# Transposing the probabilities of four heads in three chunks, the shared head put together by the transfer queue

## The reference

```
# layer 0
q, k, v = x @ Wq.T + bq, y @ Wk.T + bk, y @ Wv.T + bv
x1 = softmax(where(mask == 0, -1e9, q @ k.T)) @ v + x
# layer 1, 16 heads of 32
Q, K, V = x1 @ Wq.T + bq, ctx @ Wk.T + bk, ctx @ Wv.T + bv
attn = softmax(Q_h @ K_h.T / sqrt(32))          # for each head, 77 keys
out = LayerNorm(concat_h(attn @ V_h) @ Wo.T + bo + x1) * gamma + beta
```

## Time and profile before

| | us |
|---|---|
| median of 3 runs | 410.09 |
| lowest, highest of them | 408.79, 412.2 |
| the profiled execution, its own time | 408.65 |
| span of the profile | 406.8 |

### The profile page before, as it was taken

The page is one execution under the profiler, slowest core; times in us unless marked ns, Lnnn a source line. Parts: engine busy times, 40 slices in busy tenths (PEclk is TensorE's granted clock), DMA queues, the critical chain, the costliest instruction groups (busy, mean ns, idle before and its releaser), DMA issues.

```text
span 406.8 us, 12216 instructions
## 1 busy us (share of the span) xinstructions
PE 390.2 (96%) x4984; PEld 298.0 (73%) x4984; DVE 292.8 (72%) x711; ACT 260.7 (64%) x780; POOL 221.4 (54%) x244
## 2 busy tenths in 40 slices
PE   8999998899999999999999999999999999999894
PEld 8869856577777877777777777677777777777663
DVE  0456477548867898678967986778867986657787
ACT  2333678765678674867578567857588558766820
POOL 0420377225547755776567754765478654763541
PEclk9999999999999999999999999999999999999998
DMA  8885003400032301421041303240042200251022
GB/s 301 305 312 210 12 3 118 136 3 3 2 129 86 131 2 28 171 95 56 2 162 54 131 2 122 93 131 2 3 161 97 88 2 16 81 174 61 2 105 103
DMA packets 17302, 37.56 MB, mean 92 GB/s; under 512 B 1808, under 2 KB 3344, under 8 KB 16223
## 3 DMA queue, kind: packets, MB, share of 16 engines
q1 hardware_dynamic: 16815, 36.24, 26.0%
q10 hardware_dynamic: 432, 0.54, 0.4%
HBM read 26.49 MB, written 8.39 MB: 86 GB/s over the span
## 4 chain that ended last, share of the span: by engine, by line
PE 83%; ACT 11%; DVE 2%; DMA 2%; issue 1%; SPq 0%; DVEq 0%
PE ps_q L958 22%; PE ps_out L1023 20%; PE ps_t L983 14%; PE ps_s L972 7%; PE ps_pv L998 6%; PE ps_out L918 5%; ACT prob L503 3%; ACT pt L512 3%; ACT y L524 2%; PE ps_s L884 2%; PE ps_s L1041 2%; ACT q L467 1%; PE ps_s L897 1%; DMA raw<-in_w0k 1%; PE ps_t L1086 1%
## 5 line engine op out<-in xcount | busy, mean ns | idle before, releaser
L360 POOL TENSOR_TENSOR prob<-prob,rc 128x308 f32<-128x308 f32 x128 | 91.2, 719 | 126.0 <-DVE rc L712 125.8
L503 ACT ACTIVATE prob<-ps_s,mx 128x77 f32<-128x77 f32 x512 | 121.9, 324 | 1.8 <-DVE mx L703 1.8
L512 ACT ACTIVATE pt<-ps_t 77x512 f32<-77x512 f32 x128 | 76.2, 595 | 61.4 <-PE ps_t L983 60.9
L710 DVE TENSOR_REDUCE sm<-prob 128x4 f32<-128x308 f32 x128 | 59.5, 465 | 37.0 <-ACT prob L503 36.8
L983 PE MATMUL ps_t<-ident,prob 128*77 128x128 f32 x512 | 79.2, 277 | 3.1 <-ACT pt L512 3.1
L983 PEld LDWEIGHTS ps_t<-ident,prob 128*77 128x77 f32 x512 | 61.6, 147 | 21.5 <-issue 7.6
L703 DVE TENSOR_REDUCE mx<-ps_s 128x4 f32<-128x308 f32 x128 | 53.9, 469 | 23.1 <-PE ps_s L972 23.1
L335 POOL TENSOR_TENSOR x_l<-x_raw,x_h 128x512 fp32r<-128x512 f32 x32 | 44.6, 1398 | 21.9 <-ACT x_h L449 11.7
L958 PE MATMUL ps_q<-x_h,wq_h 128*128 128x512 f32 x128 | 53.2, 415 | 0.0
L958 PE MATMUL ps_q<-x_h,wq_l 128*128 128x512 f32 x128 | 53.0, 414 | 0.0
L972 PEld LDWEIGHTS ps_s<-k1T,q 32*64 32x64 f32 x2048 | 25.8, 130 | 27.8 <-issue 15.0
(11 more groups left out here) (130 smaller groups left out, 605.4 us busy)
## 6 DMA issues: line engine op xcount, KB each, us to landing
x_raw<-in_xT SPq DMA_DIRECT2D x8, 1024.0 KB, 7.4
y<-in_x SPq DMA_DIRECT2D x28, 256.0 KB, 2.7
out<-y SPq DMA_DIRECT2D x28, 256.0 KB, 2.0
mask_sb<-in_mask SPq DMA_DIRECT2D x8, 154.0 KB, 7.3
raw<-in_w0q SPq DMA_DIRECT2D x4, 256.0 KB, 5.9
raw<-in_w0v SPq DMA_DIRECT2D x1, 1024.0 KB, 10.1
raw<-in_w1q SPq DMA_DIRECT2D x1, 1024.0 KB, 12.7
raw<-in_w1k SPq DMA_DIRECT2D x1, 1024.0 KB, 5.0
```

Source lines behind the costliest of these rows:

```text
L360: nc.gpsimd.tensor_tensor(ap, ap, wide(rc[:, k % 2, h], KEYS), ALU.mult).then_inc(prob_done, 1)
L503: e = nc.scalar.activation(prob[:, k % 2, h, t], ps_s[:, h, t * KEYS:(t + 1) * KEYS], ACT.Exp, bias=mx[:, k % 2, h, t:t + 1])
L512: nc.scalar.activation(pt[:, h], ps_t[0:KEYS, :], ACT.Copy).then_inc(pt_ready, 1)
L710: nc.vector.reduce_sum(sm[:, k % 2, h], prob[:, k % 2, h], AX_X).then_inc(sum_done, 1)
```

## The change

The probabilities of a unit are laid out tile, head, key, so that the 4 x 77 = 308 columns of a tile lie side by side. For units 0 to 30 they are transposed as three chunks of 128, 103 and 77 columns (`CHUNK`) and not as four heads of 77. Chunk 0 holds head 0 and the first 51 keys of head 1; chunk 1 holds the other 26 keys of head 1 and then head 2; chunk 2 is head 3. Chunk c waits for POOL's scaling of head c + 1. ACT copies three chunks and not four heads.

Head 1 lies in two chunks. Two transfers on SP's queue (`gather`) bring its parts together in a new tile `pt_1`: 51 partitions from chunk 0, 26 from chunk 1. `context` waits for both (`pt_moved`). Head 2 starts 26 partitions down in chunk 1; its values are put 26 rows down in a new tile `v1_2` with zeros above, so that its matmul contracts 103 rows. `v1_2` is zeroed by POOL and filled by two transfers at the start, for which PE waits in step 1 (`v1_moved`). SP's program becomes a step for each unit too, with the same transfers as before at other places. The last unit keeps four groups of 77 columns, and copies head 1 straight to `pt_1`.

```diff
+SPLIT = P - KEYS
+CHUNKS = 3
+CHUNK = ((0, P), (P, 3 * KEYS), (3 * KEYS, GCOLS))
+SHIFT = 2 * KEYS - P
+SHIFTED = SHIFT + KEYS
...
-        pt = sb("pt", [KEYS, KC, BLOCK])
-        prob = sb("prob", [P, 2, GROUP_HEADS, TILES, KEYS])
+        pt = sb("pt", [P, CHUNKS, BLOCK])
+        pt_1 = sb("pt_1", [KEYS, BLOCK])
+        prob = sb("prob", [P, 2, TILES, GROUP_HEADS, KEYS])
...
+            sp.wait_ge(v1_ready, BATCH)
+            by_heads = v1[:].rearrange("p b (g h d) -> p b g h d", h=GROUP_HEADS, d=HEAD_DIM)
+            for v in range(BATCH):
+                sp.dma_start(v1_2[SHIFT:SHIFTED, v], by_heads[:, v, :, 2]).then_inc(v1_moved, 16)
+
+            def gather(i, k, c):
+                if not unit_exists(i, k) or k == UNITS - 1:
+                    return
+                wait(sp, pt_ready, chunks(i, k, c) + 1)
+                if c == 0:
+                    sp.dma_start(pt_1[0:SPLIT], pt[KEYS:P, 0]).then_inc(pt_moved, 16)
+                else:
+                    sp.dma_start(pt_1[SPLIT:KEYS], pt[0:SHIFT, 1]).then_inc(pt_moved, 16)
+
+            def step(i, k):
+                g, b = k % CH, k // CH
+                gather(i, k - 1, 0)
+                if g == 3:
+                    stack_probs(i, b + 1)
+                gather(i, k - 1, 1)
+                if k == 1:
+                    stack_weights(u_a, u_b, slice(1, 2), u_stacked[1], u_ready, 2)
...
+                    for t in range(TILES):
+                        load_rows(i, 0, t)
+                if g == 3:
+                    next_inputs(i, b + 1)
+                    store(i, b - 1, 0)
...
+                if g == 0:
+                    store(i, b - 2, 1)
+                if g == 1:
+                    store(i, b - 2, 2)
+                    store(i, b - 2, 3)
+                if b > 1 and k < UNITS:
+                    if g < 2:
+                        load_rows(i, b - 1, g)
+                    if g == 2:
+                        load_rows(i, b - 1, 2)
+                        load_rows(i, b - 1, 3)
...
-            def transposes(i, k, h):
+            def transposes(i, k, c):
...
-                wait(pe, prob_done, heads(i, k, h) + 1)
-                wait(pe, pt_ready, heads(i, k, h))
+                wait(pe, prob_done, heads(i, k, c + 1) + 1)
+                wait(pe, pt_ready, chunks(i, k, c))
+                n = CHUNK[c][1] - CHUNK[c][0]
                 for t in range(TILES):
-                    mm = nc.tensor.transpose(ps_t[0:KEYS, t * P:(t + 1) * P], prob[:, k % 2, h, t], ident[:])
+                    cols_of = prob[:, k % 2, t].rearrange("p h k -> p (h k)")[:, CHUNK[c][0]:CHUNK[c][1]]
+                    mm = nc.tensor.transpose(ps_t[0:n, t * P:(t + 1) * P], cols_of, ident[:])
                 mm.then_inc(t_done, 1)
...
+                if k < UNITS - 1:
+                    wait(pe, pt_ready, chunks(i, k, CHUNKS))
+                    wait(pe, pt_moved, 32 * (units(i, k) + 1))
+                    pairs = ((values(0), pt[0:KEYS, 0]), (values(1), pt_1[:]),
+                             (v1_2[:, b % 2, g], pt[0:SHIFTED, 1]), (values(3), pt[0:KEYS, 2]))
...
                 if type(i) is int and k == 1:
                     pe.wait_ge(v1_ready, BATCH)
+                    pe.wait_ge(v1_zero, 1)
+                    pe.wait_ge(v1_moved, 32)
                 transposes(i, k - 1, 0)
...
-                transposes(i, k - 1, 3)
```

More of the change, by code:

```diff
@@ L184, in units, with chunks @@
             return TURN * i + k
+        def chunks(i, k, c):
+            return CHUNKS * units(i, k) + c
         def heads(i, k, h):
@@ L265, in stored_rows, with store @@
                 return beta_done, TILES * b + t + 1
-            def store(i, b):
+            def store(i, b, t):
                 if not block_exists(i, b):
                     return
[L271 to L276, removed]
+                wait(sp, *stored_rows(b, t))
+                sp.dma_start(out[b % 2, i + b // 2, t], y[:, t, :]).then_inc(stored[t], 16)
             def move(to, frm, done):
@@ L302, in _ @@
             stack_weights(v0_a, v0_b, slice(0, BATCH), v0_stacked, v0_ready, BATCH)
[L304 to L315, removed]
+            sp.wait_ge(v1_ready, BATCH)
[18 more added lines that the diff above has]
+                    stack_weights(u_a, u_b, slice(1, 2), u_stacked[1], u_ready, 2)
+                    sp.wait_ge(mm_u, BATCH)
+                    sp.wait_ge(wq_ready, 2)
+                    sp.wait_ge(wq_l_ready, 2)
+                    for t in range(TILES):
[3 more added lines that the diff above has]
+                    store(i, b - 1, 0)
+                if g == 3 and b == LAST - 1:
                     sp.wait_ge(xl_ready, CH * BLOCKS)
@@ L319, in _ @@
                     sp.dma_start(last_y[:], last_x.rearrange("t p d -> p t d")).then_inc(ld_last, 16)
-                store(0, b - 2)
+                if g == 0:
[9 more added lines that the diff above has]
+                        load_rows(i, b - 1, 3)
+            for k in range(STEPS):
+                step(0, k)
             for t in range(TILES):
@@ L530, in step @@
                     round_ct(i, k - 2)
-                leave_pt(i, k - 1, 0)
+                transposed(i, k - 1, 0)
                 exps(i, k, 0)
@@ L534, in step @@
                     round_p0(i, b + 1)
-                leave_pt(i, k - 1, 1)
+                transposed(i, k - 1, 1)
                 exps(i, k, 1)
@@ L991, in context, with values @@
                 wait(pe, ctl_ready, units(i, k))
-                wait(pe, pt_ready, heads(i, k, GROUP_HEADS))
                 if g == 2 and block_exists(i, b + 1):
                     wait(pe, p0l_ready, blocks(i, b + 1) + 1)
-                for h in range(GROUP_HEADS):
-                    rows_of = slice(h * HEAD_DIM, (h + 1) * HEAD_DIM)
-                    own = slice(g * P + h * HEAD_DIM, g * P + (h + 1) * HEAD_DIM)
-                    mm = nc.tensor.matmul(ps_pv[rows_of, :], v1[:, b % 2, own], pt[:, h], start=True, stop=True)
+                def values(h):
+                    return v1[:, b % 2, g * P + h * HEAD_DIM:g * P + (h + 1) * HEAD_DIM]
+                if k < UNITS - 1:
[3 more added lines that the diff above has]
+                             (v1_2[:, b % 2, g], pt[0:SHIFTED, 1]), (values(3), pt[0:KEYS, 2]))
+                else:
+                    wait(pe, pt_ready, chunks(i, k, GROUP_HEADS))
+                    pairs = ((values(0), pt[0:KEYS, 0]), (values(1), pt_1[:]),
+                             (values(2), pt[0:KEYS, 1]), (values(3), pt[0:KEYS, 2]))
+                for h, (w, v) in enumerate(pairs):
+                    mm = nc.tensor.matmul(ps_pv[h * HEAD_DIM:(h + 1) * HEAD_DIM, :], w, v, start=True, stop=True)
                 mm.then_inc(pv_done, 1)
```

47 lines of the change are left out of this document (34 added, 13 removed).

## The result

| | before | after |
|---|---|---|
| median, us (20 runs each) | 410.4 | 408.26 |
| ratio of the runs, 95% interval | | 0.9908 (0.9881 to 0.9934) |
| profiled execution, own time | 408.65 | 406.01 |
| its span | 406.8 | 404.2 |
| mean granted clock | 0.996 | 0.984 |

The change gains 0.9%, 3.8 us by the ratio. The ratio leaves out runs that lie over 1.5% above the fastest of their kernel (two of 484 us before; after, six from 410.07 to 412.89 and one of 934.45), so it leans to the side of the change: the medians of all runs are only 2.1 us apart. I had forecast 401.2. The ranges of the runs overlap: the lowest after is 403.79.

The account below looks back on a forecast made before the run. PE, busy 96% of the span, was taken as the bound. The terms -12.0 + 2.0 + 1.3 + 0.6 = -8.1 took 408.65 to 400.5, 401.2 as a median; range 396.5 to 406.5.

Parts of the forecast that it names:

- What a group costs: Units 3 to 30: each dropped group of four transposes saves 0.43 us of PE, 28 x 0.43 = -12.0 us.
- What the wider chunks cost: Transposes of 128 and 103 columns: their longer weight loads fit the pace of 0.11 us, so 0.
- The wait for the moved rows in ordinary steps: Before the context: the 26 partitions land 2.0 to 3.5 us after issue, under the 4.04 of room; 0.
- the step I took for the tightest: Step 16, with g = 0: 4.47 us from ACT's second copy to the context, 4.04 without the fourth group.
- The start, unit 0: First transposes wait for two transfers of moved values, landing at 52.4: +2.0 us (1.3 to 2.8, up to 4).
- the rivals: Gate of the clock: falling to 1.2 GHz in unit 0's wait costs some 2 us more, 403.2; chance 0.2.
- Unit 1: Step 2's context: gathers behind four 256 KB row loads land at about 68.3, +1.3 us (0 to 2).
- Unit 2: Step 3: the 51-partition gather ahead of the stacking transfers starts them a little later, +0.6 us (0 to 1.5).
- SP's moved loads: SP's stores and row loads, each moved behind a gather, still have a whole step before they are needed; 0.
- no wait for `pt_1` from step 4 on: Sign expected in the profile after: from step 4 on PE never waits for the gathered rows of head 1.

Follow-up runs that it names:

- group put back: The all-late kernel with four unread transposes of 77 columns back in the old place in units 0 to 30; executed once, span 407.9 against 395.8.
- the split: The all-late kernel with each 51-partition move issued as one of 48 and one of 3 partitions; ratio to the kernel before 0.961, median 394.48.
- the filled kernel: The changed kernel, waits kept, with 13 unread matmuls before the moved-values wait and before step 2's context; ratio to the kernel before 0.9915, span 405.1.
- the split alone: The changed kernel with only each 51-partition move issued as 48 and 3; ratio to the kernel before 0.9825, span 402.4.
- the all-late kernel: The changed kernel with the moved-values wait at the first context, four row loads in step 4, last block's load behind step 28's gathers; 0.968, median 397.75.
- the kernel with the stacking first: The all-late kernel with stacking transfers ahead of both gathers in steps with g = 3; ratio to the kernel before 0.9749, span 398.4.

## Why the prediction was wrong

The direction was right, and the size was not: -8.9 forecast from median to median (410.09 to 401.2), -3.8 measured by the ratio, and 408.26 lies above the range. From profiled execution to profiled execution -8.1 was forecast (400.5) and -2.6 measured (406.01), and these 5.5 us are what the steps explain; the rest of the miss is that the changed kernel's median lies 2.25 above its profiled execution, where I had allowed 0.7. By its steps:

- **What a group costs.** Right: -11.6 forecast for steps 4 to 30, -11.7 measured even with new waits in it, and 0.43 to 0.44 for each group put back in three steps of four. In steps with g = 3 the group is about half of the gain, and the rest was counted as 0; the sum does not show it.
- **What the wider chunks cost.** Right: nothing. The pair of weight loads in the earlier trace rows was the row to read, though it overstated the load of 128 columns (144 ns, not 190).
- **The wait for the moved rows in ordinary steps.** Right for the contexts of steps 4 to 27, 29 and 30; step 31 waits 0.60. It has less room than the step I took for the tightest: in the kernel before 3.77 from the end of ACT's second copy to the context, against 4.47 in step 16. Not seen: the gather of 51 partitions stands ahead of the stacking transfers in each step with g = 3. I had counted this for unit 2 alone. It is cheap later on: two of the six later steps wait, 0.57 us in all, and the steps take 10.62 in the mean, against 10.48 with the split. The waits of about 0.5 that the expectations speak of are those of the weight load, which matmuls mostly cover.
- **The start, unit 0.** Mis-sized: +2.0 forecast, +3.6 measured. The landing was taken at 52.4, 4.39 behind the scores, and PE went on 4.40 behind them, so the wait was sized well: with the clock kept up step 1 is 1.8 longer than before. The rest is the clock: 1.75 by the filled kernel. It stood among the rivals at a chance of 0.2 and a price of 2, when the row at the end, a fall within 3 us of idleness, against a wait forecast at 3.5 called for a place in the sum.
- **Unit 1.** This is the step that failed most: +1.3 forecast, +3.8 measured. The mechanism was the one named, gathers behind four row loads, but I let them land at 68.3, 8.7 us into step 2, and PE went on 10.5 into it (73.98 less 63.50): a landing 1.7 too early, and the loss of clock, 0.85 in this step, put at nothing. I gave the gathers the time of a small transfer behind the bulk rows. In the trace few engines are busy at the end of PE's wait:

```profile
71.00:72.00 1.00, 0.00 (x0) 0.00 (x0) 0.75 (x3) 0.24 (x1) 1.00 (x1) 1.00 0.21 80
72.00:73.00 1.00, 0.00 (x0) 0.00 (x0) 0.00 (x0) 0.00 (x0) 1.00 (x3) 1.00 0.13 51
```

With the split alone PE went on 8.85 into the step (71.94 less 63.09), close to the 8.7. But the shape is not the whole cause: with the 51-partition gather as it was and only the first wait moved, PE went on 9.08 into the step (68.81 less 59.73). In both of these the four row loads took 1.87 us to issue; in the changed kernel they took 2.38, so that the gathers were issued 0.5 later, and in the filled kernel, which is as late (10.52), 2.83. Where the rest of the 1.7 comes from is open.

- **Unit 2.** +0.6 forecast, +1.9 measured: the stacking wait rose from 0.72 to 1.11, and the step began with the clock down. The two do not add up. With the clock kept up in steps 1 and 2, step 3 still takes 11.4, with a wait of 2.04: the late rows set its length. With the split alone they are in time and it takes 9.6, although the clock is down at its start; with the clock full as well it takes 8.9.
- **SP's moved loads.** Taken at 0, wrong in one place: the last block's 1 MB load is now issued ahead of the gathers of step 28, which cost 1.08 there, and up to 2.6 in other runs. So the sign "no wait for `pt_1` from step 4 on" did not hold, in steps 28 and 31.

The changed kernel scatters from 403.8 to 412.9 in 19 runs (and one of 934), where the kernel with all loads late and the split stays within 393.6 to 395.1 in four. That the scatter comes from how often and where the clock falls is my reading. The mean granted clocks point that way, 0.983 to 0.990 in the eight runs under 407 us and 0.977 to 0.985 in the six over 410, and the filled kernel's five runs lie within 2.2 us; no run proves it.

## What to carry to other kernels

Before a piece of data is sent through the transfer queue, list every bulk transfer that can stand ahead of it, at the start and the end of the program too, and put the wait at the first reader. Here three misplaced orders and one awkward shape hid 11 us of a gain of 14 (spans of 404.2, 393.1 and 406.8). A new wait on a busy TensorE costs its own length and, behind most of the longer ones here, the clock as well (1.75 us behind the one of 3.45); both belong in the sum. And a total that fits is not yet a term that fits: compare step by step, as the group put back shows.

## What was not expected of the hardware

- A move of 51 partitions of 2 KB within SBUF keeps only three DMA engines busy (share 0.19), and splitting it into 48 and 3 gains 2.7 us of span over the kernel (395.8 to 393.1), in spite of 39 more transfers.
- The clock fell behind waits much shorter than the 3.5 us of step 1: in the all-late kernel the longest wait near the fall was 1.79 us, and in the one with the fourth group back 1.57. In the kernel with the stacking first, waits of 0.95 and 1.83 close together left it at 1.00 over the same stretch. What decides between the two stays open.
- Weight loads of 128 columns of fp32 in front of a moving operand of only 128 columns cost nothing beside loads of 77, and in these transposes they last 144 ns, less than the 172 of 103 columns.
